# One ring of four PSUM banks for the first attention layer, and other places of work in its order

## The reference

```python
B, M, N, DIM, DH, H = (8, 1024, 64, 256, 128, 8)     # here 512 latents, 512 + 512 keys
xn = _layernorm(x, gamma_media, beta_media)
ln = _layernorm(latents, gamma_lat, beta_lat)
q = ln @ Wq + bq
kv = jnp.concatenate([xn, ln], axis=1) @ Wkv + bkv
k, v = jnp.split(kv, 2, axis=-1)
sim = jnp.einsum('bhid,bhjd->bhij', q * DH ** (-0.5), k)
attn = jax.nn.softmax(sim, axis=-1)
out = jnp.einsum('bhij,bhjd->bhid', attn, v)
return out.transpose(0, 2, 1, 3).reshape(b, -1, INNER) @ Wo + bo
```

## Time and profile before

| | us |
|---|---|
| median of 3 runs | 3115.68 (3115.3 to 3116.95) |
| profiled execution, its own time | 3124.96 |
| span of the profiled execution | 3123.3 |
| attention of layer 0 within it | 34.6 to about 1592 |
| TensorE busy in the span | 2865.7 (92%) |
| VectorE, ScalarE, GpSimd busy | 2241.8, 1799.2, 1706.6 |

### The profile page before, as it was taken

How to read it: one execution, slowest core, us unless ns; L and a number is a source line. 1 busy time by engine, 2 the same in 40 slices (tenths; PEclk the granted TensorE clock), 3 DMA queues, 4 the chain that set the end, 5 groups by cost and what they waited for, 6 DMA issues and landing times. The chain is left out here.

```text
span 3123.3 us, 46820 instructions
## 1 busy us (share of the span) xinstructions
PE 2865.7 (92%) x17032; PEld 2286.6 (73%) x17032; DVE 2241.8 (72%) x3546; ACT 1799.2 (58%) x2774; POOL 1706.6 (55%) x1054
## 2 busy tenths in 40 slices
PE   6999999999999999999959958999999976999999
PEld 5777877778777877877849944555555445999999
DVE  6777777777777777777745547777777635578887
ACT  3555555555545555455525526888888853366665
POOL 3543544435444354443334426888887743568886
PEclk9999999999999999999979978999999988999999
DMA  5654333333333433333245634444433122368885
GB/s 150 211 180 127 98 119 91 112 124 96 119 96 110 126 92 118 98 106 114 81 150 202 218 106 140 117 122 123 123 116 95 49 87 97 106 184 236 226 236 147
DMA packets 295880, 409.73 MB, mean 131 GB/s; under 512 B 30323, under 2 KB 216850, under 8 KB 295664
## 3 DMA queue, kind: packets, MB, share of 16 engines
q1 hardware_dynamic: 274864, 375.28, 37.9%
q0 software_dynamic: 18656, 29.00, 4.8%
q10 hardware_dynamic: 2144, 2.62, 0.3%
HBM read 259.51 MB, written 149.04 MB: 131 GB/s over the span
## 5 line engine op out<-in xcount | busy, mean ns | idle before, releaser
L1789 POOL TENSOR_TENSOR c_pT_lo<-c_prob,c_pT_hi 128x1024 fp32r<-128x1024 f32 x192 | 456.4, 2384 | 115.6 <-ACT c_pT_hi L1872 111.6
L482 ACT ACTIVATE a_prob<-a_scores,a_neg_max 128x1024 f32<-128x1024 f32 x256 | 285.7, 1116 | 396.9 <-DVE a_neg_max L606 396.9
L403 POOL TENSOR_TENSOR a_pT_lo<-a_turned,a_pT_hi 128x1024 fp32r<-128x1024 f32 x64 | 152.7, 2386 | 656.1 <-ACT a_pT_hi L474 656.1
L606 DVE TENSOR_REDUCE a_neg_max<-a_scores 128x1 f32<-128x1024 f32 x256 | 309.9, 1211 | 90.5 <-PE a_scores L36 87.5
L1984 DVE TENSOR_REDUCE c_neg_max<-c_max 128x2 f32<-128x1024 f32 x248 | 302.2, 1219 | 72.6 <-PE c_max L2217 71.5
L1866 ACT ACTIVATE c_prob<-c_scores 128x1024 f32<-128x1024 f32 x256 | 261.3, 1021 | 72.5 <-PE c_scores L2228 67.9
L34 PE MATMUL m_h<-m_rT_hi,m_w_hi 128*128 128x256 f32 x880 | 253.8, 288 | 2.3 <-DVE m_rT_lo L2718 1.9
L35 PE MATMUL m_h<-m_rT_lo,m_w_hi 128*128 128x256 f32 x880 | 248.9, 283 | 1.0 <-issue 1.0
L36 PE MATMUL m_h<-m_rT_hi,m_w_lo 128*128 128x256 f32 x880 | 248.6, 282 | 0.7 <-issue 0.7
L34 PE MATMUL a_pj<-a_pT_hi,a_v_hi 128*128 128x512 f32 x512 | 208.0, 406 | 43.9 <-DVE a_qT_lo L538 40.6
L2613 POOL TENSOR_TENSOR m_w_lo<-m_w_in,m_w_hi 128x1024 fp32r<-128x1024 f32 x80 | 201.6, 2520 | 59.0 <-ACT m_w_hi L2661 58.6
(11 more groups left out here) (354 smaller groups left out, 9182.4 us busy)
## 6 DMA issues: line engine op xcount, KB each, us to landing
m_w_in<-L_ffn_w_in SPq DMA_DIRECT2D x117, 512.0 KB
blocks_dram<-a_turned SPq DMA_DIRECT2D x64, 512.0 KB, 2.6
a_turned<-blocks_dram SPq DMA_DIRECT2D x256, 128.0 KB, 2.9
blocks_dram<-a_prob SPq DMA_DIRECT2D x64, 512.0 KB, 3.1
a_prob<-blocks_dram SPq DMA_DIRECT2D x256, 128.0 KB, 3.0
e_w_in<-L_ffn_w_in SPq DMA_DIRECT2D x32, 1024.0 KB, 7.6
qk_dram<-c_stage SPq DMA_DIRECT2D x64, 256.0 KB
c_q_rows<-qk_dram SPq DMA_DIRECT2D x32, 512.0 KB, 5.1
```

Of the source, the lines that this page charges most:

```text
L403: g.tensor_tensor(by_query(pT[1], t), from_blocks(staged[t]), by_query(pT[0], t).bitcast(F32), ALU.subtract).then_inc(turned_lo, 1)
L482: a(prob[:, qt, :], ps_s[:, qt % 2, :], ACT.Exp, bias=neg_max[:, qt:qt + 1], accum_out=row_sum[:, par, qt:qt + 1]).then_inc(exp_done, 1)
L606: ve.tensor_reduce(neg_max[:, qt:qt + 1], ps_s[:, qt % 2, :], AX.X, ALU.max, negate=True).then_inc(max_done, 1)
L1789: g.tensor_tensor(flat(pT[1][:, kt - 1]), flat(prob[:, kt]), flat(pT[0][:, kt - 1]).bitcast(F32), ALU.subtract).then_inc(lo_pool, 1)
```

## The change

`a_pj` has four banks (`RING = 4`), and `a_probT` is gone: `turn2` and `turn3` become the steps `left2 right2` and `left3 right3`, each of one bank of that ring, with the same eight transposes of TensorE in the same place. TensorE now waits for the use four before. The copy of two bias columns to `a_qk_bias` before each head is gone, since the projections read `bias` itself. In the string `tr0` moves behind `scores1`, `tr1` ahead of `scores2`, `hi0` ahead of `scores3`, and `hi1`, in even heads, between `v1` and `v2`; in the last head of a batch `tr0` moves behind `pro0`. VectorE's routing and statistics parts move one step ahead. The two new waits of TensorE (`LAID`) take the place of what the two banks had implied. The sync engine's and GpSimd's programs stay as they were.

```diff
-                steps = "scores0 turn3 tr0 qk0 qk1 scores1 fin0 scores2 tr1 fin1 scores3 qk2 v0 hi0 v1 v2 out0 turn2 hi1 v3 out1"
+                steps = "scores0 turn3 qk0 qk1 scores1 tr0 fin0 tr1 scores2 fin1 hi0 scores3 qk2 v0 v1 hi1 v2 out0 turn2 v3 out1"
...
-                steps = "scores0 turn3 tr0 qk0 scores1 fin0 scores2 tr1 fin1 scores3 qk1 hi0 qk2 out0 turn2 out1 hi1"
+                steps = "scores0 turn3 qk0 scores1 tr0 fin0 tr1 scores2 fin1 hi0 scores3 qk1 qk2 out0 turn2 hi1 out1"
...
-                steps = "scores0 turn3 tr0 pro2 scores1 pro3 scores2 pro0 tr1 fin0 scores3 fin1 qk0 pro1 hi0 qk2 out0 qk1 turn2 out1 hi1"
+                steps = "scores0 turn3 pro2 scores1 pro3 scores2 pro0 tr0 fin0 tr1 scores3 fin1 qk0 pro1 hi0 qk2 out0 qk1 turn2 hi1 out1"
...
+            for qt in "23":
+                steps = steps.replace("turn" + qt, "left" + qt + " right" + qt)
...
-                if kind == "qk" and j == 0:
-                    act.wait_ge(qk_bias_set, n + 2)
...
-                if n < 8 * B - 1:
-                    set_qk_bias((n + 1) % H0, 1 - par)
...
             def free_bank(u):
-                if not (isinstance(u, int) and u < 2):
-                    pe.wait_ge(pj_out, u - 1)
+                if u >= RING:
+                    pe.wait_ge(pj_out, u - RING + 1)
...
+                if kind == "qk" and (n, int(j != 1)) in LAID:
+                    pe.wait_ge(pj_out, LAID[n, int(j != 1)])
...
+                elif kind in TURNS:
+                    for k in range(4):
+                        kt = 4 * TURNS.index(kind) + k
+                        last = t.transpose(dst[:, k * P:(k + 1) * P], prob[:, j, kt * P:(kt + 1) * P], ident[:])
```

More of the change, by code:

```diff
@@ L126, in layer0_attention @@
         set_up = sem("set_up")
-        qk_bias_set = sem("qk_bias_set")
         x_load = sem("x_load")
@@ L213, in layer0_attention @@
                 KEYS_DONE[n + 1] = START[n] + max(uses.index(("qk", 1)), uses.index(("qk", 2))) + 1
+            for j in range(1, 4, 2):
+                if ("pro", j) in uses:
+                    LAID[n, j // 2] = START[n] + uses.index(("pro", j)) + 1
+            for qt in range(2, TB):
+                if ("right", qt) in uses:
+                    TURNED[n - (qt == 3), qt] = START[n] + uses.index(("right", qt)) + 1
             for use in (("zt", 1), ("lg", 0), ("cn", 0)):
@@ L508, in step @@
                     elif is_use((kind, j)):
-                        use_bank((kind, j), u, u % 2, n, par, b + 1)
+                        use_bank((kind, j), u, u % RING, n, par, b + 1)
                         u += 1
-                    if late is not None:
+                    if late is not None and kind != "left":
                         exp(n, late, par)
@@ L525, in _ @@
             batches(act, pair)
-            prob_high(8 * B - 1, 3)
-            use_bank(("fin", 1), START[8 * B], START[8 * B] % 2, 8 * B, 0, 0)
+            for i, use in enumerate((("left", 3), ("right", 3), ("fin", 1))):
+                use_bank(use, START[8 * B] + i, (START[8 * B] + i) % RING, 8 * B, 0, 0)
         @block.vector
@@ L731, in step @@
                             route_add_up(route, dve, b - 1)
-                    elif after == ("scores", 3):
+                    elif after == ("scores", 2):
                         if at == (0, 1) and not b:
@@ L744, in step @@
                             route_number_rows(route, dve, b - 1)
-                        elif at == (3, 1) and b:
+                    elif after == ("scores", 3):
+                        if at == (3, 1) and b:
                             route_locate(route, dve, b - 1)
@@ L755, in _ @@
             invert_sums(n - 1, 1)
[L756 to L759, removed]
+            for i, use in enumerate((("left", 3), ("right", 3), ("fin", 1), ("out", 0), ("out", 1))):
+                use_bank(use, u + i, HIGH_START[n] + i, (u + i) % RING, n, 0, 0)
         @block.tensor
@@ L846, in scores @@
                 last.then_inc(s_full, 1)
-            def turn(n, qt):
-                pe.wait_ge(exp_done, 4 * n + qt + 1)
-                for half in range(2):
-                    m = 4 * n + 2 * qt - 4 + half
-                    if not (isinstance(m, int) and m < 2):
-                        pe.wait_ge(t_out, m - 1)
-                    for k in range(4):
-                        kt = 4 * half + k
-                        last = t.transpose(ps_t[:, half, k * P:(k + 1) * P], prob[:, qt, kt * P:(kt + 1) * P], ident[:])
-                    last.then_inc(t_full, 1)
             pe.wait_ge(K.filled, 9)
@@ L888, in _ @@
             n, u = 8 * B, START[8 * B]
-            turn(n - 1, 3)
-            for part in range(2):
-                use_bank(("fin", part), u, u % 2, n, 0, B, 4)
-            for j in range(2):
-                use_bank(("out", j), u + 1 + j, (u + 1 + j) % 2, n, 0, B, 4)
+            for i, use in enumerate((("left", 3), ("right", 3), ("fin", 0), ("fin", 1), ("out", 0), ("out", 1))):
+                at = u + i - (i > 2)
+                use_bank(use, at, at % RING, n, 0, B, 4)
 E0, F0 = 16, 1024
```

82 lines of the change are left out of this document (35 added, 47 removed).

## The result

The changed kernel takes 3196.93 us (median of 4 runs, 3193.79 to 3205.43), the one before 3115.49 (3115.22 to 3116.95): a ratio of 1.0265, 95% interval 1.0243 to 1.0286. It is slower by 81 us. The forecast was 3162, slower by 46, in a range of 3100 to 3195: the direction is right, the time lies just outside.

A forecast was written before the change was run, and what follows sets the result against it. TensorE bounds, held up by a chain over ScalarE and VectorE that two banks cannot cover. Waits +22 and clock +24 make 46 on the profiled 3124.96, so 3171, or 3162 us on the median; range 3100 to 3195.

The forecast's parts named there:

- Bound, and what four banks remove: TensorE bounds, held up by two banks; with four, the waits ahead of `fin0` go and head 31 falls to 21.1 us.
- The sum of 12.45 us: TensorE's idle time in one batch of eight heads, about 100 us over eight batches: all the change could take away.
- The copy ("I take nothing for it by itself"): Removing VectorE's bias copy, 63 times 1.01 us, moves nothing on TensorE while the banks hold; without that cover, 64 us.
- Where tile 1 goes: Tile 1's way over DRAM: written 13.3 us into an odd head, reads 3.7 later, ScalarE's `hi1` 4.6 after the reads.
- the third rival: Faster by far: tile 1 lands before 20 us, so `hi1` does not hold `v2` up; 3050 us, chance 0.08.
- The waits' sum: Four pairs of heads change by +4.1, +1.2, -2.4 and +0.6 us; with last batch, start and tail, +22 in all.
- The clock: Gaps ahead of `v3` drop TensorE to 1.2 GHz in seven heads like 30 and half of seven like 28: +24 us.
- the fifth rival: Slower still: every even head falls to the slow clock, 22 + 31 x 2.4 = +96, 3212 us; chance 0.07.
- From the profile to the median: The sum on the profiled execution, 3171 us, is taken to the median, 0.3% lower: 3162.
- The first: Rival: the same as the forecast without a fall of TensorE's clock, 3138 us; chance 0.27.
- the second: Rival: faster because the way over DRAM is short and `hi1` lands sooner in each pair, 3106 us; chance 0.12.
- fourth: Rival: no difference, as head 31's gain of 27 us and the even heads' loss cancel, 3116 us; chance 0.08.

The follow-up runs named there:

- Kernel 5: The changed kernel with the six order strings of before, so the ring of four and the bias in place but no step moved: 3023.71 us, ratio 0.9701.
- kernel 6: The kernel before without its copies of the bias, which ScalarE and VectorE read in place: 3076.18 us, ratio 0.9862.
- kernel 9: The changed kernel with the two copies of the bias put back on VectorE: 3208.97 us, ratio 1.0297 to the kernel before.
- kernel 4: The changed kernel with 12 matmuls whose result nothing reads ahead of each `v3` in even heads: 3188.53 us, ratio 1.0224 to the kernel before.
- Kernel 1: The changed kernel with `hi1` of even heads behind `turn2` again: 3056.41 us, ratio 0.9791 to the kernel before.
- kernels 3 and 7: 3: changed kernel, weights' loads behind both tiles' write and reads on the sync queue, 3106.49 us; 7: that and `hi1` of even heads behind `turn2`, 3023.55 us.

## Why the forecast was right in direction and short in size

The forecast is 35 us short of the measured median. Three terms make it up: the clock 14 us, the waits 9, and the step from the profile to the median 12. The time lies only 2 us above the range, so each of the three alone decided between inside and outside. The largest, and the one whose reasoning was wrong, is the clock.

**Bound, and what four banks remove: right, and under-used.** No wait for the lo part of the queries is left, head 31 is at 21.16 us (21.1 forecast). Kernel 5 shows what the sum did not: without the moves the ring and the bias give 92 to 96 us. The forecast had this inside the even heads' length, which the landing overrules, so the total did not depend on it; but a reader of it would take the ring for a small thing. One reading of the earlier trace rows was wrong: the idle time is 1.4 us in head 24 alone; heads 28 and 30 have 1.7 and 0.75. The sum of 12.45 us stands.

**The copy ("I take nothing for it by itself"): wrong** for the kernel before (43 us, kernel 6), where the sentence's own condition, "while the banks hold", was not met; in the changed one it is 10 to 12 us (kernel 9).

**Where tile 1 goes: right.** By ScalarE's and the queue's timelines, medians over the seven or eight heads of a kind: write of tile 1 13.6 us into head 29's kind (13.3), write to reads 3.6 (3.7), reads to ScalarE 4.3 (4.6; in head 27's kind it is 6.4, since ScalarE comes to `hi1` after the tile has landed), `hi1` of the odd head 21.5 in (21.6), from it to `hi1` of the even head 23.9 (24.1). At full clock the head then ends 4.54 later (4.58). The argument against the third rival misread: there the write of tile 1 in head 31 left 11.3 us in, under the 13 that it names. In the even heads, which that rival is about, the writes of the changed kernel left 14.5 to 17.8 us in (medians of each kind).

**The waits' sum: nearly right.** The profiled spans differ by 68.9 us. Without the 37.6 of the clock behind `hi1` that leaves 31, where +22 was forecast. Most of the difference is head 27's kind, 24.0 us in place of 22.5, whose clock fell as well; of the forecast's four gaps ahead of `v3`, 5.5, 4.2, 3.7 and 3.0 in heads 30, 28, 32 and 26, the medians of the idle time in TensorE's timeline were 5.4, 4.0, 3.3 and 2.6 (batches 1 to 7). The forecast's own lengths give 5.8 and 4.4 for the first two.

**The clock: this is the step that failed.** The forecast let seven heads like 30 fall and half of the seven like 28, at 2.4 us each: +24. It was 26 of 31: all 14 heads of these two kinds in the first seven batches, and 12 of the 15 like 24 and 26, for which the forecast had none. A fall cost 1.78 us at most and 1.4 on average: 37.6. So the count was far too low and the price too high, and the two errors partly cancel: 26 falls at 2.4 would be 62. I had drawn a line at the one gap of 4.11 us that the earlier trace rows showed. One row that fell gives no line below which nothing falls. The changed trace has none either: the clock did not fall in head 32, behind 3.27 us, and did in head 58, behind 2.48, the shortest gap of a head that fell (timeline, then windows from `hi1` to the head's end):

```profile
875.36 0.38 PE L34 MATMUL a_pj<-a_wv_hi,a_kvT_hi 128*128 128x256 f32 x1 [3.27 <-DVE a_v_lo L537]
...
1535.44 0.39 PE L34 MATMUL a_pj<-a_wv_hi,a_kvT_hi 128*128 128x256 f32 x1 [2.48 <-DVE a_v_lo L537]
```

```profile
873.04:877.59 4.55, 2.23 (x18) 2.23 (x19) 2.53 (x5) 3.03 (x5) 2.37 (x1) 1.00 0.03 5
1533.12:1539.20 6.08, 3.76 (x19) 3.76 (x20) 3.17 (x6) 3.11 (x5) 2.36 (x1) 0.72 0.00 0
```

That the falls are worth 37.6 us of the whole time is a sum over stretches, not an experiment: kernel 4 took 24.7 of it away and gained 8 to 13.

The rule of the Trainium skill, page "TensorE: Matmul & The Clock Gate", part 1, that the slow clock is the default and activity releases it, spoke for the fifth rival, all even heads, at 3212 us with a chance of 0.07. The trace agrees in part: five even heads did not fall. Of all the cases this one still came nearest, in the count of heads and in the time, though it too had the price of a fall too high. It should have held more.

**From the profile to the median: 9 to 12 us.** The forecast took 0.3% off the sum, since the profiled execution of before lay that much over its median. The profiled run of the changed kernel lay 3 us under its median. So between medians the kernels differ by 81 us, between profiles by 69. The kernel before ran in 3115 to 3127 us beside the experiments, so this term is scatter between executions and no step of the working.

**The rivals.** The first (3138, no fall) is excluded by the windows, the second and fourth by the landing, the third by ScalarE's wait of 5.58 us. Kernel 1, at 3056, comes near the third's 3050 us by the way that it named: `hi1` no longer holds `v2`.

## What to carry to other kernels

Where an engine empties PSUM in a written order, keep an instruction that waits for a DMA behind the evictions whose banks are needed soon: counted from its place behind `turn2`, the same instruction cost 141 us ahead of `v2` and 42 behind it. When a change has several parts, build the one that only adds room, here the ring in the old order: it is 173 us faster than the whole. And look at what stands on the queue ahead of the late transfer: a wait for something else and two loads held it for 1 to 3 us in a head, and 90 us of the time hung on that.

## What the runs showed of the hardware

Half clock cost time here only where TensorE was what was waited for. In the changed kernel 34 stretches of the attention, 164 us in sum by the clock's record, stood at half speed; taking 21 of them away (kernel 4) gave 8 to 11 us of time (medians, spans).

The clock fell behind gaps that I would not have called long. In head 27 of the changed kernel TensorE idled 0.78 us, then did 16 matmuls of 16 columns, and at their end the clock fell (windows, head 27 in parts):

```profile
734.00:737.80 3.80, 3.80 (x19) 2.80 (x17) 2.04 (x3) 1.70 (x3) 2.75 (x6) 1.00 0.49 147
737.80:741.30 3.50, 2.72 (x19) 2.58 (x19) 2.10 (x4) 2.15 (x3) 1.26 (x1) 0.88 0.68 215
741.30:744.70 3.40, 3.40 (x11) 2.62 (x10) 0.66 (x1) 0.69 (x1) 1.10 (x1) 0.62 0.55 154
744.70:747.40 2.70, 2.70 (x23) 2.42 (x21) 1.62 (x4) 1.89 (x4) 0.00 (x0) 1.00 0.00 0
```

The same work in the kernel before kept 1.00 throughout; there the idle time ahead of the 16 matmuls was 0.19 us. With 0.76 to 0.82 us ahead of them the clock fell in all of the six heads of this kind in batches 1 to 6 of the changed kernel, in 3 of the six in kernel 1, and in 1 of the six in each of kernels 3 and 7; in kernel 1 it fell in head 59 too, where that idle time was 0.19. In heads of the kind of 26, too, a gap of 2.74 us was followed by half clock (head 26) and one of 2.77 by full clock (head 42). What decides between them stays open.
